# The norm ahead of the second layer in two halves: tiles 0 to 15 are normalised while tiles 16 to 31 are still being added

## The chip, the cores and the metric

The kernel runs on one core of a Trainium2 chip. The metric is the time of one execution on the device in microseconds (us). The kernel before takes 1013.03 us, the median of 3 runs (1012.9 to 1013.12).

## The reference, cut to what matters

The program is four layers of a transformer with 4096 tokens of width 128 (`x` is 64x64x128). Each layer is an attention against a context and a second part that differs from layer to layer. Around the change it computes

```
x = x + L0_attention(layernorm(x), ctx, ctx, tau, delta)     # 16 heads of width 8
x = x + L0_ffn(layernorm(x), g_info, W_qkv, W_proj, b_proj)  # self-attention over x with a class per token
```

where `layernorm(x) = (x - mean) / sqrt(var + 1e-5)` over the 128 columns of a token. The change touches the second of these norms and the step that makes the queries from it. All arithmetic stays as it is.

## The kernel before, in words

The 4096 tokens lie in the array `X` as 32 tiles of 128 tokens; four tiles are a chunk (512 tokens), so there are 8 chunks. Attention runs over 16 units of two tiles. Each engine has its own program, and the programs meet at semaphores; inside one engine the order is that of the code.

**Attention of layer 0.** In the DVE program, turn u of `attention` does the maxima and shifts of unit u, then `values(u - 1)` (reciprocal of the denominators, rows of the output), then `update(u - 2)`, which adds the projected output of two tiles to `X`, and then the statistics of two tiles (`tile_stats`, line 872) one turn later. Three more turns (u = 16, 17, 18) drain this pipe. In turn 16 DVE also does `windows()` and `guides()` (lines 846 to 864), small preparations for later layers. ACT does the exponentials and copies the turned weights and outputs out of PSUM (lines 1798, 1837, 1805); its program has turns 16 and 17. PE ends its program with 18 matmuls that compute nothing that is used (`keep_clock`, line 2077).

**The norm between.** `norms(1)` of DVE waits for the statistics of all 32 tiles, works out the variance (lines 909 to 915, five instructions of 128x32), waits for the square root of ACT (`rstds(1)`, line 1727) and makes the reciprocal root and one Newton step (lines 919 to 932). The result is a scale and a shift for each token (`rstd`, `nmr`). In front of its root ACT computes an Exp for a later layer (line 1896), and between the two stands a load of ACT's function table.

**The queries of layer 0's second part** (`prepare_own` of DVE and ACT, `prepare(1, 1, KT)` of PE). ACT normalises the four tiles of a chunk into one of two buffers (line 1741); PE turns them into the PSUM bank `psT` or `psY`, in turn (line 2115); DVE copies the bank to `KT` (line 1363); PE multiplies it by the query weights (line 2124); DVE writes the queries to `QT` (line 1367). POOL squares each chunk of queries (line 715), and when all 8 are there PE begins the classes of the tokens (line 2561).

Of the kernel before, what the change touches and what calls it, by code (L numbers as in the profile page):

```python
# [8 lines left out]
ACT = mybir.ActivationFunctionType  # L9
# [10 lines left out]
TILES = TOK // 128  # L20
CHUNK = 512
CHUNKS = TOK // CHUNK
# [6 lines left out]
WINDOW, DEV_POW = 16.0, 128.0  # L29
# [85 lines left out]
def build(nc, a, out):  # L115
    ctx = ExitStack()
    with ctx:
# [320 lines left out]
        KEEP_AT, BEST_AT, RANK_AT = {8: 0, 12: 1, 14: 2, 16: 3}, {9: 0, 13: 1, 15: 2, 17: 3}, {10: 0, 14: 1, 16: 2}  # L438
        PAIR_AT, PAIRS = 3, 15
        CHAIN_STEPS = 7  # L440
        NORM_AT = [0, 1, 2, 3, 4, 6, 7]
        gauss_ready = sem("gauss_ready")
        g_loaded = sem("g_loaded")
        sim_step = sem("sim_step")
# [375 lines left out]
        def _(v):  # L820
# [163 lines left out]
            def attention(l):  # L984
                wb = units_before[l]
                masked = l == 1

                def scores(u):
                    n = wb + u
                    sc = ps_sc[:, :].rearrange("p (r g k) -> p r g k", r=RG, k=S)  # L990
                    pr = P_s[u % 2].rearrange("p (t r i k) -> p t r i k", t=2, r=RG, k=S)
                    v.wait_ge(scores_ready, n + 1)
                    for t in range(2):
                        v.tensor_reduce(mx4[:, :, HPR * t:HPR * t + HPR], sc[:, :, HPR * t:HPR * t + HPR], AX.X,  # L994
                                        ALU.max).then_inc(max_ready, 1)
                    if masked and u >= 2:
                        mix_registers(u - 2)
                    if l == 3 and u in (4, 6, 8, 10, 12, 14):
                        four_variances((u - 4) // 2)

                    wait_reuse(v, p_turned, 4 * (n - 1))
                    for t in range(2):
                        g = slice(HPR * t, HPR * t + HPR)
                        v.wait_ge(max_ready, 2 * n + t + 1)
                        v.tensor_tensor(pr[:, t], sc[:, :, g], mx4[:, :, g].unsqueeze(3).broadcast_to([128, RG, HPR, S]),  # L1005
                                        ALU.subtract).then_inc(shifted, 1)

                def values(u):
                    n = wb + u
                    o = psT[:, 0:288].rearrange("p (g d) -> p g d", d=E + 1)  # L1010
                    v.wait_ge(pv_ready, n + 1)
                    if u < UNITS - 1:
                        keep_and_rank(u + 1)
                    v.reciprocal(rden[:, :], o[:, :, E]).then_inc(rden_ready, 1)
                    v.wait_ge(rden_ready, n + 1)

                    wait_reuse(v, o_turned, n)
                    v.tensor_tensor(o_rows[:, :].rearrange("p (g d) -> p g d", d=E), o[:, :, 0:E],
                                    rden[:, :].unsqueeze(2).broadcast_to([128, 2 * H, E]), ALU.mult).then_inc(ots_ready, 1)

                def keep_and_rank(u):
                    if l == 3 and u == UNITS - 1:
                        v.wait_ge(counted, 2)
                        v.tensor_copy(ei[:, 0, :], count_at).then_inc(place_step, 1)
                    if l == 3 and u in KEEP_AT:
                        keep_logits(KEEP_AT[u])
                    if l == 3 and u in RANK_AT:
                        rank_of(1, RANK_AT[u], rank_at(RANK_AT[u]))

                def mix_registers(u):  # L1030
                    of_reg = ots[:, :].rearrange("p (b s) -> p b s", s=S)[:, :, 0:REG]
                    v.wait_ge(o_evac, wb + u + 1)
                    v.scalar_tensor_tensor(of_reg, of_reg, 0.5, reg_out[:, UNIT * u:UNIT * u + UNIT, :],
                                           ALU.mult, ALU.add).then_inc(ots_mixed, 1)

                def update(u):
                    n = wb + u
                    t = 2 * u
                    v.wait_ge(y_ready, n + 1)
                    v.wait_ge(bo_added, TILES * l + t + 2)  # L1040
                    xt = X[:, t:t + 2, :]
                    v.tensor_tensor(xt, psY[:, 0:256].rearrange("p (t d) -> p t d", d=D), xt, ALU.add).then_inc(x_updated, 2)

                def finish_registers():
                    v.wait_ge(reg_kept, REG_STEPS)
                    v.reciprocal(reg_all[:, :, 1, :], reg_all[:, :, 1, :]).then_inc(reg_rden, 1)
                    v.wait_ge(reg_rden, 1)
                    v.tensor_tensor(reg_out[:, :, :].rearrange("p (k b) q -> p k (b q)", b=4), reg_all[:, :, 0, :],
                                    reg_all[:, :, 1, :], ALU.mult).then_inc(reg_ready, 1)
                    v.wait_ge(reg_ready, 1)  # L1050

                for u in range(UNITS + 3 if l < 3 else UNITS):
                    if u < UNITS:
                        scores(u)
                        if masked and u == 0:
                            finish_registers()
                    elif l == 0 and u == UNITS:
                        windows()
                        guides()
                    elif masked and u < UNITS + 2:  # L1060
                        mix_registers(u - 2)
                    if l == 3 and u in (4, 6, 8, 10, 12, 14):
                        four_norms((u - 4) // 2)
                    if l == 3 and u in BEST_AT:
                        best_of(1, BEST_AT[u])
                    if 1 <= u <= UNITS:
                        values(u - 1)
                    if 2 <= u <= UNITS + 1:
                        update(u - 2)
                    if l == 3 and u in RANK_AT:  # L1070
                        place(1, RANK_AT[u])
                    if l == 3 and u == UNITS - 1:
                        early_rows_table()
                    behind = 2 if l == 3 else 3
                    if behind <= u < UNITS + behind:
                        for t in (2 * (u - behind), 2 * (u - behind) + 1):
                            tile_stats(UPD_OF[l] + 1, t)
                if l == 3:
                    four_variances(6)
                    early_shifts()  # L1080
                    four_norms(6)
                return values, update
# [273 lines left out]
                unrolled(REG_STEPS, 2, step)  # L1356

            def prepare_own():

                def step(k, turn, u, live):  # L1360
                    if live(0):
                        v.wait_ge(xt_in_psum, CHUNKS + k + 1)
                        v.tensor_copy(KT[:, bass.ds(k * CHUNK, CHUNK)], (psT, psY)[u][:, :]).then_inc(xt_ready, 1)
                    if live(1):
                        r = (u + 1) % 2
                        v.wait_ge(q_proj, CHUNKS + k)
                        v.tensor_scalar(QT[:, bass.ds((k - 1) * CHUNK, CHUNK)], psS[r][:, :], bqkv[:, 1, 0:1],
                                        float(E) ** -0.5, ALU.add, ALU.mult).then_inc(q_ready, 1)

                pipeline(v, CHUNKS, 2, 1, step)  # L1370

            for t in range(TILES):
                tile_stats(0, t)
# [5 lines left out]
                            bo[:, :, :].rearrange("p l d -> p (l d)"), ALU.add).then_inc(bo_ready, 1)  # L1379
            prepare(0, 0, tau_s)  # L1380
            attention(0)
            norms(1)
            prepare_own()
            classes()
            registers()
# [50 lines left out]
            def mixture1():  # L1436
# [15 lines left out]
                                            two[:, :, NE:], be[:, :].unsqueeze(1).broadcast_to([128, 2, D]),  # L1452
                                            ALU.add).then_inc(y_kept, 1)

                v.wait_ge(norm_ready, 2 * 3 + 2)
                pipeline(v, CHUNKS, 2, 2, step)
                routing()

# [263 lines left out]
        def _(act):  # L1722
# [9 lines left out]

            def normalise(ln, k, u):

                if isinstance(k, int) and (k == 0 or k == 4 and ln in (4, 6)):
                    act.wait_ge(norm_ready, 2 * (NORM_AT[ln] + k // 4) + 2)
                wait_reuse(act, xt_in_psum, CHUNKS * ln + k - 1)
                tiles = TPC // 2 if ln in SHARED_LN else TPC
# [23 lines left out]
                act.activation(xts[s][:, :], (psT, psY)[s][:, :], ACT.Copy).then_inc(xt_ready, 1)  # L1762

            def prepare_own():
                pipeline(act, CHUNKS, 2, 0, lambda k, turn, u, live: normalise(1, k, u))

            def prepare(ln, last_keys, between=None):
                def step(k, turn, u, live):
# [22 lines left out]
            def attention(l):  # L1791
# [52 lines left out]
                for u in range(UNITS + 2 if l < 3 else UNITS + 1):  # L1844
                    if 1 <= u <= UNITS:
                        turned(u - 1)
                    elif u > UNITS:
                        outputs(u)
                    if l == 2 and u == UNITS:
                        act.preload_act_table_set("sqrt_and_others")  # L1850
                    if u < UNITS:
                        exponentials(u)

# [38 lines left out]
                    rstds(0)  # L1892
            prepare(0, lambda: take_all(0, CHUNKS - 1))
            attention(0)
            act.wait_ge(gcol_step, 2)
            act.activation(gcols[:, 1, :], gcols[:, 1, :], ACT.Exp, scale=-1.0 / DEV_POW).then_inc(gauss_ready, 1)
            rstds(1)
            prepare_own()
            classes()
            registers()  # L1900
# [169 lines left out]
        def _(pe):  # L2070
# [35 lines left out]
            def prepare(l, ln, kept=None):  # L2106
                w = W[l]

                def step(k, turn, u, live):
                    s = u % 2  # L2110
                    if live(0):
                        normalised(ln, k)
                        wait_reuse(pe, xt_ready, CHUNKS * ln + k - 1)
                        for j in range(TPC):
# [18 lines left out]
            def attention(l):  # L2133
# [134 lines left out]
                        values(u - 1, 2)  # L2268
                        values(u - 1, 3)
                if l == 0:  # L2270
                    keep_clock(psS[0], 18)
                elif l == 2:
                    pe.wait_ge(l2_loaded, 80)
                    keep_clock(psS[0], 4)
# [437 lines left out]
```

## Time and profile before

| | us |
|---|---|
| median of 3 runs | 1013.03 |
| the profiled execution, its own time | 1013.32 |
| its span | 1011.5 |
| PE busy in the span | 909.9 |
| DVE busy | 751.1 |
| ACT busy | 578.3 |

The profile is that of one execution. Starts are counted from the start of its span; what lies around the span is 1.8 us. A row of the timeline gives the start, the time from the start of the first to the end of the last of the merged instructions, the engine, the line, what is written from what, and in brackets the idle time of that engine before the row with the instruction that ended it. The stretch that the change touches goes from about 153 us (turn 16 of the attention) to 181.5 us (the classes begin).

### The profile page before, as it was taken

What the parts mean: (1) busy time and instruction counts of PE and PEld (TensorE: products, weight loads), DVE (VectorE), ACT (ScalarE), POOL (GpSimd) and SP (SyncE); (2) the same over time, 40 slices, a digit from 0 to 9 for tenths busy, and PEclk for the clock granted to TensorE, in tenths of its full rate; (3) what the DMA queues carried; (4) which work ended last, traced back from release to release, by engine and by line L of the source; (5) the groups of instructions that cost most, each with busy time, mean ns of one, the idle gap of its engine ahead of it and who ended that gap; (6) DMA issues with size and microseconds to landing.
All of it is one profiled execution on the core that took longest, in us unless ns stands there. A gap on an engine that the chain in (4) does not pass through costs nothing.

```text
span 1011.5 us, 32199 instructions
## 1 busy us (share of the span) xinstructions
PE 909.9 (90%) x12735; PEld 704.4 (70%) x12735; DVE 751.1 (74%) x1744; ACT 578.3 (57%) x1200; POOL 390.8 (39%) x435
## 2 busy tenths in 40 slices
PE   6899998988899998999987989989898998879897
PEld 3467885465777764788755857578854887668896
DVE  3588995556899956999789766556567999876664
ACT  4656666543566656666646763235485666433454
POOL 5234421335334211444202006735564435547554
PEclk9999999989999999999999999999999999798999
DMA  8399000000000000000099811122230111122221
GB/s 268 93 333 279 3 3 1 2 8 4 3 3 2 3 2 1 3 3 3 3 299 295 208 42 35 46 62 77 67 93 1 45 44 54 44 78 57 56 64 35
DMA packets 73695, 68.83 MB, mean 68 GB/s; under 512 B 7565, under 2 KB 68944, under 8 KB 73552
## 3 DMA queue, kind: packets, MB, share of 16 engines
q1 hardware_dynamic: 68336, 57.60, 20.4%
q0 software_dynamic: 4544, 8.94, 2.7%
q8 instruction: 103, 1.69, 0.7%
q14 instruction: 40, 0.33, 0.1%
q10 hardware_dynamic: 672, 0.27, 0.1%
HBM read 22.36 MB, written 44.67 MB: 66 GB/s over the span
## 4 chain that ended last, share of the span: by engine, by line
PE 28%; DVE 12%; issue 4%; ACT 3%; another core or an unknown queue 1%; POOL 1%; DMA 1%; DVEq 1%; POOLq 0%; SPq 0%; ACTq 0%
PE ps_sc L2517 7%; PE ps_pt L2525 4%; PE ps_sc L2452 2%; DVE work L1005 2%; PE ps_pt L2461 1%; PE ps_pt L2178 1%; PE psT L2192 1%; DVE stats L872 1%; DVE mx L994 1%; PE ps_sc L2166 1%; PE ps_pt L2093 1%; PE ps_sc L2088 1%; POOL xs_dram L703 1%; PE ps_pt L2443 1%
## 5 line engine op out<-in xcount | busy, mean ns | idle before, releaser
L1837 ACT ACTIVATE P_t<-ps_pt 128x512 f32<-128x512 f32 x256 | 140.0, 594 | 146.6 <-PE ps_pt L2178 140.2
L994 DVE TENSOR_REDUCE mx<-ps_sc 128x16 f32<-128x1024 f32 x128 | 150.2, 1215 | 19.4 <-PE ps_sc L2166 19.2
L2192 PE MATMUL psT<-VB,P_t 128*64 128x18 f32 x4096 | 145.3, 213 | 13.7 <-ACT P_t L1837 6.3
L2192 PEld LDWEIGHTS psT<-VB,P_t 128*64 128x64 f32 x4096 | 131.9, 138 | 35.6 <-ACT P_t L1837 25.8
L1005 DVE TENSOR_TENSOR work<-ps_sc,mx 128x1024 f32<-128x1024 f32 x128 | 150.1, 1214 | 0.0
L1798 ACT ACTIVATE work<-work 128x1024 f32<-128x1024 f32 x128 | 130.9, 1058 | 27.9 <-DVE work L1005 26.2
L2178 PE MATMUL ps_pt<-cst,work 128*128 128x128 f32 x1024 | 142.2, 283 | 0.0
L2178 PEld LDWEIGHTS ps_pt<-cst,work 128*128 128x128 f32 x1024 | 112.2, 143 | 26.7 <-ACT work L1798 20.6
L656 POOL TENSOR_TENSOR kbh<-KT,cst 128x512 f32<-128x512 f32 x64 | 65.3, 1042 | 134.7 <-PE ps_sc L2166 93.8
L656 POOL TENSOR_TENSOR rt<-KT,cst 128x512 f32<-128x512 f32 x64 | 65.5, 1045 | 101.5 <-PE ps_sc L2166 101.5
L2517 PE MATMUL ps_sc<-kbh,KT 128*128 128x128 f32 x624 | 89.4, 289 | 2.1 <-DVE kbh L1633 1.2
L2517 PEld LDWEIGHTS ps_sc<-kbh,KT 128*128 128x128 f32 x624 | 79.8, 200 | 6.7 <-DVE kbh L1633 3.6
L2043 ACT ACTIVATE P_t<-ps_sc,KT 128x128 f32<-128x128 f32 x156 | 44.6, 368 | 55.0 <-PE ps_sc L2517 47.8
L2525 PE MATMUL ps_pt<-VB,P_t 128*128 x468 | 68.4, 284 | 6.5 <-DVE P_t L1638 5.2
L2525 PEld LDWEIGHTS ps_pt<-VB,P_t 128*128 128x128 f32 x468 | 60.7, 198 | 8.8 <-issue 8.4
L663 POOL TENSOR_TENSOR x_rows<-x_rows,bo 128x256 f32<-128x256 f32 x64 | 43.5, 683 | 45.7 <-issue 26.4
L872 DVE BATCH_NORM_STATS2 stats<-x_rows 128x6 f32<-128x128 f32 x256 | 56.9, 280 | 4.4 <-DMA x_rows<-x_in 3.7
L703 POOL DMA_INDIRECT xs_dram<-QT,dest x32 | 31.1, 973 | 70.3 <-issue 68.3
L797 POOL DMA_INDIRECT ys_dram<-work,to_row x39 | 37.9, 973 | 39.8 <-DVE to_row L1626 19.2
L1605 DVE COPY KT<-VB 128x512 f32 (+1 forms) x78 | 34.8, 446 | 23.4 <-ACT P_t L2043 16.6
L799 POOL DMA_INDIRECT out<-work,to_row x39 | 39.0, 1000 | 34.0 <-issue 16.5
L1741 ACT ACTIVATE work<-x_rows,nmr,rstd 128x128 f32<-128x128 f32 (+1 forms) x112 | 46.8, 483 | 7.1 <-DVE nmr L932 3.0
(374 smaller groups left out, 1716.9 us busy)
## 6 DMA issues: line engine op xcount, KB each, us to landing
xs_dram<-slots SPq DMA_DIRECT2D x1, 17292.0 KB, 71.0
xs_dram<-slots SPq DMA_DIRECT2D x1, 17160.0 KB, 58.6
ctxT<-xs_dram SPq DMA_DIRECT2D x39, 65.5 KB
work<-xs_dram SPq DMA_DIRECT2D x39, 65.0 KB
VB<-L_ffn_W1b_in SPq DMA_DIRECT2D x8, 258.0 KB
ctxT<-ctxT_in SPq DMA_DIRECT2D x4, 512.0 KB, 6.9
x_rows<-x_in SPq DMA_DIRECT2D x4, 512.0 KB, 9.2
QT<-ys_dram SPq DMA_DIRECT2D x4, 512.0 KB, 6.1
```

Source lines behind the costliest of these rows:

```text
L656: pool.tensor_tensor(by_head[:, 2 * h:2 * h + 2, :, :], KT[:, at:at + 2 * S].rearrange("p (b k) -> p b k", k=S).unsqueeze(2).broadcast_to( ...
L872: v.bn_stats(stats[:, bass.ds(t, 1), :].rearrange("p o c -> p (o c)"), X[:, bass.ds(t, 1), :].rearrange("p o d -> p (o d)")).then_inc(stat ...
L994: v.tensor_reduce(mx4[:, :, HPR * t:HPR * t + HPR], sc[:, :, HPR * t:HPR * t + HPR], AX.X, ALU.max).then_inc(max_ready, 1)
L1005: v.tensor_tensor(pr[:, t], sc[:, :, g], mx4[:, :, g].unsqueeze(3).broadcast_to([128, RG, HPR, S]), ALU.subtract).then_inc(shifted, 1)
L1741: act.activation(xn[u][:, j, :], X[:, bass.ds(t, 1), :].rearrange("p o d -> p (o d)"), ACT.Identity, bias=nmr[:, bass.ds(t, 1)], scale=rst ...
L1798: act.activation(half_p, half_p, ACT.Exp).then_inc(exp_ready, 1)
L1837: act.activation(P_t[:, 512 * c:512 * c + 512], ps_pt[:, 512 * (c % 2):512 * (c % 2) + 512], ACT.Copy).then_inc(p_evac, 1)
L2043: done = act.activation(hT[s][:, cols], psS[s][:, cols], ACT.Relu, bias=w_tile[s][:, 512 + j:513 + j])
L2178: mm = pe.transpose(ps_pt[:, 512 * (c % 2) + 128 * r:512 * (c % 2) + 128 * r + 128], P_s[u % 2][:, at:at + 128], ident)
L2192: mm = pe.matmul(psT[64 * b:64 * b + 64, 144 * t + 18 * g:144 * t + 18 * g + 18], P_t[:, at:at + 64], VB[:, UNIT * u + 2 * t + b, g, :, :] ...
L2517: mm = pe.matmul(psS[r][:, 128 * b:128 * b + 128], w_tile[r][:, 128 * b:128 * b + 128], xT[r], start=True, stop=True)
L2525: mm = pe.matmul(psO[s][:, 0:128], hT[s][:, 128 * b:128 * b + 128], wv[:, bass.ds(e_back * F + (w_out_at + 128 * b), 128)], start=(b == 0) ...
```

## The change

The norm is made in two halves. The variance of tiles 0 to 15 is worked out in turn 16 of the attention, ahead of `windows()`, and its reciprocal root at the end of that turn, ahead of the last `update`. ACT's Exp, the table load and the root of the first half move up into turn 16, ahead of the last copy of outputs. The variance of tiles 16 to 31 comes where `norms(1)` stood; its root is taken by ACT between chunks 1 and 2, and its reciprocal root by DVE between the copies of chunks 0 and 1. ACT waits for the second half at chunk 4. `prepare_own` is unrolled on both engines. PE waits for the end of `psT`'s use ahead of chunk 0 and for the last `update` ahead of chunk 1 (these hold `psT` and `psY`), and its `keep_clock` behind the attention goes from 18 matmuls to 6. The numbering of the norms' semaphores moves by one for the later norms.

```diff
-        NORM_AT = [0, 1, 2, 3, 4, 6, 7]
+        NORM_AT = [0, 1, 3, 4, 5, 7, 8]
 # DVE, attention
                 for u in range(UNITS + 3 if l < 3 else UNITS):
+                    if l == 0 and u == UNITS:
+                        finish_first = norms_of(1, slice(0, TILES // 2), 0)
                     if u < UNITS:
                         scores(u)
...
                         for t in (2 * (u - behind), 2 * (u - behind) + 1):
                             tile_stats(UPD_OF[l] + 1, t)
+                    if l == 0 and u == UNITS:
+                        finish_first()
 # DVE, prepare_own
+                finish_second = norms_of(1, slice(TILES // 2, TILES), 1)
+
+                def take_own(k, u):
+                    v.wait_ge(xt_in_psum, CHUNKS + k + 1)
+                    v.tensor_copy(KT[:, bass.ds(k * CHUNK, CHUNK)], (psT, psY)[u][:, :]).then_inc(xt_ready, 1)
+
+                take_own(0, 0)
+                finish_second()
...
-                    if live(0):
-                        v.wait_ge(xt_in_psum, CHUNKS + k + 1)
-                        v.tensor_copy(KT[:, bass.ds(k * CHUNK, CHUNK)], (psT, psY)[u][:, :]).then_inc(xt_ready, 1)
+                    if live(0) and k > 0:
+                        take_own(k, u)
...
-                pipeline(v, CHUNKS, 2, 1, step)
+                unrolled(CHUNKS, 1, step)
...
             attention(0)
-            norms(1)
             prepare_own()
 # ACT
-                if isinstance(k, int) and (k == 0 or k == 4 and ln in (4, 6)):
+                if isinstance(k, int) and (k == 0 or k == 4 and ln in (1, 4, 6)):
...
-                pipeline(act, CHUNKS, 2, 0, lambda k, turn, u, live: normalise(1, k, u))
+                for k in range(CHUNKS):
+                    normalise(1, k, k % 2)
+                    if k == 1:
+                        root_of(1, slice(TILES // 2, TILES), 1)
...
-                    if l == 2 and u == UNITS:
+                    if l == 0 and u == UNITS:
+                        act.wait_ge(gcol_step, 2)
+                        act.activation(gcols[:, 1, :], gcols[:, 1, :], ACT.Exp, scale=-1.0 / DEV_POW).then_inc(gauss_ready, 1)
+                    if l in (0, 2) and u == UNITS:
                         act.preload_act_table_set("sqrt_and_others")
+                    if l == 0 and u == UNITS:
+                        root_of(1, slice(0, TILES // 2), 0)
...
             attention(0)
-            act.wait_ge(gcol_step, 2)
-            act.activation(gcols[:, 1, :], gcols[:, 1, :], ACT.Exp, scale=-1.0 / DEV_POW).then_inc(gauss_ready, 1)
-            rstds(1)
             prepare_own()
 # PE, prepare
                     if live(0):
+                        if l == 1 and isinstance(k, int) and k == 0:
+                            pe.wait_ge(ots_ready, UNITS)
+                        elif l == 1 and isinstance(k, int) and k == 1:
+                            pe.wait_ge(x_updated, TILES)
                         normalised(ln, k)
 # PE, end of attention
                 if l == 0:
-                    keep_clock(psS[0], 18)
+                    keep_clock(psS[0], 6)
```

## Rows read from the trace of the kernel before

**Rows 1.** Chain that ended last: shares of the span by engine.

```profile
PE 28%; DVE 12%; issue 4%; ACT 3%; another core or an unknown queue 1%; POOL 1%; DMA 1%; DVEq 1%; POOLq 0%; SPq 0%; ACTq 0%
```

**Rows 2.** Timeline of ACT, 155 to 190 us: start, length, work, idle before.

```profile
155.94 1.08 ACT L1837 ACTIVATE P_t<-ps_pt 128x512 f32<-128x512 f32 x2 [1.04 <-PE ps_pt L2178]
159.62 0.38 ACT L1805 ACTIVATE oh<-psY 128x256 f32<-128x256 f32 x1 [2.59 <-PE psY L2203]
159.90 0.22 ACT L1896 ACTIVATE gcols<-gcols 128x32 f32<-128x32 f32 x1
160.14 1.28 ACT L1727 ACT_TABLE_LOAD   x1
162.93 0.23 ACT L1727 ACTIVATE lnw<-lnw 128x32 f32<-128x32 f32 x1 [1.51 <-DVE lnw L915]
164.48 7.94 ACT L1741 ACTIVATE work<-x_rows,nmr,rstd 128x128 f32<-128x128 f32 x20 [1.32 <-DVE nmr L932]
172.90 4.73 ACT L1741 ACTIVATE work<-x_rows,nmr,rstd 128x128 f32 x12 [0.47 <-PE psY L2115]
```

**Rows 3.** Timeline of DVE, 153 to 185 us.

```profile
157.88 0.36 DVE L1014 RECIPROCAL rden<-psT 128x32 f32<-128x32 f32 x1 [2.82 <-PE psT L2192]
...
158.94 0.48 DVE L872 BATCH_NORM_STATS2 stats<-x_rows 128x6 f32<-128x128 f32 x2
160.86 0.43 DVE L1042 TENSOR_TENSOR x_rows<-psY,x_rows 128x256 f32<-128x256 f32 x1 [1.44 <-issue]
161.20 0.86 DVE L872 BATCH_NORM_STATS2 stats<-x_rows 128x6 f32<-128x128 f32 x4
162.10 0.22 DVE L909 TENSOR_TENSOR lnw<-stats 128x32 f32<-128x32 f32 x1
...
164.25 0.19 DVE L932 SCALAR_TENSOR_TENSOR nmr<-lnw,rstd 128x32 f32<-128x32 f32 x1
166.88 0.69 DVE L1363 COPY KT<-psT 128x512 f32<-128x512 f32 x1 [2.44 <-PE psT L2115]
```

**Rows 4.** Timeline of PE, 157 to 186 us.

```profile
160.60 4.05 PE L2077 MATMUL ps_sc<-cst 128*128 128x512 bf16 x18
166.18 0.66 PE L2115 MATMUL psT<-cst,work 128*128 128x128 f32 x4 [1.53 <-ACT work L1741]
...
169.48 1.06 PE L2115 MATMUL psT<-cst,work 128*128 128x128 f32 x4
170.34 1.88 PE L2124 MATMUL ps_sc<-KT,W 128*128 x2
...
178.28 1.02 PE L2124 MATMUL ps_sc<-KT,W 128*128 x2
...
181.54 1.92 PE L2561 MATMUL ps_sc<-QT,gate 128*32 128x512 f32 x16 [0.73 <-DVE QT L1367]
```

**Rows 5.** PE by stretches: length, busy (x instructions), granted clock, DMA share, GB/s.

```profile
165.24:168.65 3.41, 1.59 (x10) 1.00 0.00 0
168.65:172.06 3.41, 3.41 (x9) 0.50 0.00 0
...
202.78:206.20 3.42, 0.80 (x22) 1.00 0.05 8
206.20:209.61 3.41, 3.19 (x69) 0.50 0.05 8
```

**Rows 6.** Timeline of DVE, 758 to 762 us: the same chain over 16 tiles.

```profile
760.08 0.24 DVE L919 RECIPROCAL lnw<-lnw 128x16 f32<-128x16 f32 x1
...
760.99 0.17 DVE L932 SCALAR_TENSOR_TENSOR nmr<-lnw,rstd 128x16 f32<-128x16 f32 x1
```

**Rows 7.** ACT at other places: roots of 16 tiles (min/median/max ns); a table load.

```profile
L1731 ACT ACTIVATE lnw<-lnw x4: 198/216/217, 543.0 to 759.0; 128x16 f32<-128x16 f32 x4
...
600.09 1.28 ACT L2002 ACT_TABLE_LOAD   x1 [1.31 <-DVE nmr L932]
601.39 1.65 ACT L1989 ACTIVATE QT<-x_rows,nmr,rstd 128x128 f32<-128x128 f32 x4
```

More of the change, by code:

```diff
@@ L1453, in step @@
                                             ALU.add).then_inc(y_kept, 1)
-                v.wait_ge(norm_ready, 2 * 3 + 2)
+                v.wait_ge(norm_ready, 2 * NORM_AT[3] + 2)
                 pipeline(v, CHUNKS, 2, 2, step)
```

## The prediction

> **What bounds the kernel now.** I read the chain of waits first. PE has the largest share of it, 28%, DVE 12% and ACT 3% [rows 1], so no single engine is the bound everywhere and the stretch has to be read for itself. I then read the three timelines from turn 16 of the attention to the start of the classes.
>
> The stretch is one chain. The last two tiles are added at 160.86 us; four statistics follow (161.20), the variance (162.10), ACT's root (162.93 to 163.16), and the Newton step ends at 164.25 + 0.19 = 164.44 [rows 2, 3]. ACT starts on the first tile at 164.48, released by `nmr`, and is then busy nearly without a gap: 20 tiles in 7.94 us, 0.47 us idle, 12 tiles in 4.73 us, so its last tile ends at 177.63 [rows 2]. The classes start on PE at 181.54, released by the last queries of DVE; that is 3.91 us behind ACT's last tile [rows 4]. So ACT, at 0.397 us for a tile and 1.59 us for a chunk, sets the pace here, and the end of the stretch is the start of ACT's stream plus its work plus a tail. No tile of the first 16 needs anything that happens after 159.42, the end of the statistics of turn 16 (158.94 + 0.48) [rows 3]. The wait is one for all statistics, not one for data.
>
> **The change part by part.**
>
> First variance (five instructions, DVE, turn 16). With 32 tiles it takes from 162.10 to the start of ACT's root at 162.93, 0.83 us [rows 2, 3]; half as many columns won't take longer. It stands ahead of `windows()`, and DVE is idle for 2.82 us at the end of that work, until PE has the last values at 157.88 [rows 3]. 0.83 fits in 2.82, so it costs nothing; without that cover it would cost at most 0.83. Behind it on DVE stand `windows()` and `guides()`, and ACT's Exp waits for two of these; ACT is free only at 155.94 + 1.08 = 157.02 [rows 2], later than they are done.
>
> Exp, table load and first root (ACT, turn 16). Exp takes 0.22, the load 1.28 [rows 2], a root over 16 tiles 0.22 [rows 7]: 1.72 us, say 1.8 with the gaps. ACT is idle for 2.59 us from 157.02 until the turned outputs of the last unit release it at 159.62 [rows 2]. So it is done at about 158.8, with 0.8 to spare. Behind these three waits the last copy of outputs, and for that copy wait PE's projection and the last update: each us beyond the cover is paid in full.
>
> The Trainium skill, "ScalarE: Activation LUTs", section "What ACT_TABLE_LOAD costs", speaks against this fit: a switch of the set costs the load and a drain of about 1.38 us, 2.66 us in all. The rows do not show such a drain: behind the load at 600.09, 1.28 long, the next activation starts at 601.39 [rows 7]. By the page ACT would be done at 157.02 + 0.22 + 2.66 + 0.22 = 160.12, past its cover, and the gain would be some 0.7 us smaller; this is a rival below, worked there from the rows.
>
> First reciprocal root (five instructions, DVE). Over 16 tiles it goes from 760.08 to 760.99 + 0.17, 1.08 us [rows 6]. It starts behind the statistics of turn 16, at 159.42 + 0.04, and ends at 160.54. DVE is idle there for 1.44 us, until the last update at 160.86 [rows 3], so this is hidden too, with 0.3 to spare; the update does not move. Nothing else waits behind it.
>
> Start of ACT's stream. It becomes 160.54 + 0.04 = 160.58 instead of 164.48: 3.90 us earlier. ACT has by then done its last copy of outputs (159.62 + 0.38 = 160.00) [rows 2]. This is the main term.
>
> Second half. Its variance comes where the old one stood, 162.10 to at most 162.93 [rows 3], while ACT works on chunks 0 and 1 until 160.58 + 8 x 0.397 = 163.76. ACT then takes the second root, 0.22 us, less a few hundredths by which activations overlap: I charge 0.20. DVE copies chunk 0 at about 163.0, waits for the root until 164.0 and has the second half at 165.1. So its copy of chunk 1, which could have started at 166.88 + 1.53 - 3.90, about 164.5, is 0.6 to 0.7 late. What hides this: the next work of PE is to turn chunk 2, which ACT finishes only at 163.96 + 1.59 = 165.55; the copy (0.69 us [rows 3]) is through at 165.8, and the projection of chunk 1 stands behind the turning in any case. Without that cover it costs 0.7. ACT needs the second half for chunk 4, at 163.96 + 3.18 = 167.1, two us after it is there.
>
> PE. Its new waits are for the last rows of outputs, made before the statistics at 158.94, and for the last update, at 160.86 + 0.43 = 161.29 [rows 3], both before chunk 0 is normalised (160.58 + 1.59 = 162.17). `keep_clock` must shrink for this: 18 matmuls take 4.05 us from 160.60 [rows 4] and would hold PE until 164.65; 6 take 1.35 and end at 161.95, 0.2 ahead of chunk 0. PE then waits as it did before, from chunk to chunk.
>
> The clock of PE. In the stretch 165.24 to 168.65 PE was busy for 1.59 of 3.41 us, and in the next one the granted clock was 0.50, the lower level of 1.2 GHz [rows 5]. There, turning a chunk takes 1.06 instead of 0.66 and projecting it 1.88 instead of 1.02 us [rows 4], together 2.94, more than ACT's 1.59; ACT's idle 0.47 us [rows 2], ended by PE's turning, is what came of it. In the changed kernel the gap behind the last `keep_clock` matmul is 0.2 to 0.4 us instead of 1.53, so PE has more to do in such a stretch. I take it that the clock stays at 2.4 GHz here and the 0.47 us go; at the other end they stay.
>
> Unrolled loops. ACT's 0.397 us for a tile holds across its loop and the part in front of it [rows 2], so the loop cost nothing that could be won; I set 0, between -0.1 and 0.1.
>
> Numbers of the norms' semaphores: 0, a constant in an instruction that is there anyway.
>
> Sum: 3.90 - 0.20 + 0.47 = 4.17 us; 3.70 if the idle time stays. Behind 181.54 all waits for the last queries [rows 4], so I carry the gain to the end at its full size. From the profiled execution, 1013.32 - 4.17 = 1009.15; its time is 0.29 above the median of the runs, so for the median 1013.03 - 4.17 = 1008.86, **1008.9 us**.
>
> **The rivals.**
>
> The clock falls at the new place, for longer. With 12 matmuls fewer PE may be found too little busy while chunks 0 and 1 come in, and run the next chunks at 1.2 GHz, two low stretches instead of one. Each holds 3.41/2.94, about 1.2 chunks, each 1.35 us over ACT's pace: 1.6 us a stretch, of which before only 0.47 came through since the other engines had slack. For two I take 3.2 less 1.2 of slack, 2.0 us, from a base of 4.17: gain 2.2, 1010.8 us. For it speaks that the first pair of chunks still leaves PE idle for some 0.9 us of each 1.59 (turning takes 0.66) [rows 4]; against it that the long gap is gone.
>
> The table load holds ACT for longer than it shows. If the root comes out at 160.12, DVE makes the first half from 160.16 to 161.24, ACT starts at 161.28, 0.70 later than forecast, and the update, 0.5 late, lies beside that. Gain 3.5, 1009.5 us. Against it stands the load with an activation 0.02 us behind it [rows 7].
>
> The clock further down. All that follows moves by 4 us, and the gaps of PE that cost it the clock later, such as 0.80 busy of 3.42 us ahead of the fall at 206.20 [rows 5], fall differently. One low stretch more or less, with PE at the bound, is worth up to half of its 3.41 us, 1.7 us either way: 1007.2 or 1010.6 us.
>
> The gain does not arrive. Should something that the change does not move set the start of the classes or of what follows them, the time stays 1013.0. Against it: PE's wait at 181.54 was ended by DVE's queries, and nothing else is named there [rows 4].
>
> The other side: PE stays at 1.2 GHz through the whole preparation, because with waits at every chunk it is never busy enough to be given 2.4 GHz. It would cost 8 chunks x 1.35 = 10.8 us against the forecast, 1019.7 us. It decides from about three chunks on (4.17/1.35). Against it: at the low clock PE was busy for 3.41 of 3.41 us, and the clock rose at once [rows 4, 5]: a slower PE has no gaps here.
>
> **How the numbers follow.** Forecast 0.60; longer fall of the clock 0.15; table load 0.05; clock further down by more than 1 us 0.12 (half to each side); gain does not arrive 0.05; PE slow throughout 0.03. The forecast's own range is 1008.4 to 1009.5 (the idle 0.47 stays or goes, 0.1 for loops). To leave out no more than 2 in 10 I go from 1007.5 to 1011.0: below it half of the better cases further down, above it the last two rivals and part of two others. A measurement of this kernel can tell about 0.2%, 2.0 us, from no change: faster means under 1011.0. Forecast, table load, nearly all of the clock cases: faster 0.85; within 0.2%: 0.11, the gain that does not arrive and the worse ends of the clock cases; slower 0.04.
>
> **What would show it.** Right: ACT's Exp, load and root lie between 157.0 and 158.9 and the copy of outputs still starts at about 159.6; the last update stays at 160.9; ACT's first tile starts at about 160.6, its last ends at 173.5; the classes start at 177.4; PE's clock is 1.00 from 161 to 177. Wrong: a copy of outputs after 159.8 (load), a clock of 0.50 for more than 3.4 us before 177 (PE), an idle gap of ACT behind the second root, or a start of the classes at 177.4 with a span that is not 4 us shorter (further down).

## The result, and the profile after

The changed kernel takes 1006.09 us, the median of 20 executions (1001.78 to 1012.69). The kernel before, measured beside it, takes 1009.61 us, also of 20 (1006.95 to 1015.23); the three runs that the prediction started from are among these. The ratio is 0.9961, with a 95% interval of 0.9943 to 0.9978: faster by 0.4%. (The ratios in this document are those of the measurement; the quotient of the two medians, here 0.9965, can differ from them by up to 0.0016.) The forecast was 1008.9 us in a range from 1007.5 to 1011.0; the measured median lies below it. The forecast as a ratio, 1008.86/1013.03 = 0.9959, was met. One execution in the whole study, of the kernel late_half below, was slow (1447.36 us at a mean granted clock of 0.548); it is left out of that kernel's median and ratio.

The profiled execution of the changed kernel took 1002.57 us (span 1000.8), 10.7 us less in span than the one of before. The timeline of ACT from 154.9 us on (start, length, work, idle before) answers to [rows 2]:

```profile
154.98 1.28 ACT L1866 ACT_TABLE_LOAD   x1
156.27 0.22 ACT L1741 ACTIVATE lnw<-lnw 128x16 f32<-128x16 f32 x1
157.43 0.38 ACT L1818 ACTIVATE oh<-psY 128x256 f32<-128x256 f32 x1 [0.95 <-PE psY L2222]
158.26 3.19 ACT L1751 ACTIVATE work<-x_rows,nmr,rstd 128x128 f32<-128x128 f32 x8 [0.44 <-DVE nmr L932]
161.35 0.20 ACT L1741 ACTIVATE lnw<-lnw 128x16 f32<-128x16 f32 x1
161.46 9.33 ACT L1751 ACTIVATE work<-x_rows,nmr,rstd 128x128 f32<-128x128 f32 x24
```

Load and root lie ahead of the copy of outputs at 157.43, with 0.95 us to spare. The stream of tiles has no idle time: it ends at 161.46 + 9.33 = 170.79. DVE, against [rows 3]:

```profile
155.69 0.36 DVE L1014 RECIPROCAL rden<-psT 128x32 f32<-128x32 f32 x1 [2.21 <-PE psT L2211]
...
158.05 0.18 DVE L932 SCALAR_TENSOR_TENSOR nmr<-lnw,rstd 128x16 f32<-128x16 f32 x1
158.68 0.43 DVE L1042 TENSOR_TENSOR x_rows<-psY,x_rows 128x256 f32<-128x256 f32 x1 [0.45 <-PE psY L2233]
...
160.68 0.69 DVE L1367 COPY KT<-psT 128x512 f32<-128x512 f32 x1
161.59 0.25 DVE L919 RECIPROCAL lnw<-lnw 128x16 f32<-128x16 f32 x1 [0.22 <-ACT lnw L1741]
...
162.59 0.69 DVE L1367 COPY KT<-psY 128x512 f32<-128x512 f32 x1
```

The first half is ready at 158.23, 0.45 us ahead of the last update, which is still released by PE's projection. PE, against [rows 4]:

```profile
158.42 1.46 PE L2092 MATMUL ps_sc<-cst 128*128 128x512 bf16 x6
160.01 0.63 PE L2134 MATMUL psT<-cst,work 128*128 128x128 f32 x4
161.55 0.63 PE L2134 MATMUL psY<-cst,work 128*128 128x128 f32 x4 [0.91 <-issue]
...
163.22 0.65 PE L2134 MATMUL psT<-cst,work 128*128 128x128 f32 x4 [0.19 <-ACT work L1751]
163.71 1.02 PE L2143 MATMUL ps_sc<-KT,W 128*128 x2
...
174.30 1.92 PE L2580 MATMUL ps_sc<-QT,gate 128*32 128x512 f32 x16 [0.73 <-DVE QT L1378]
```

The stretches of PE (length, busy and instructions, granted clock, DMA) answer to [rows 5]: the fall in the preparation is gone, the one at the register step is still there.

```profile
158.50:161.91 3.41, 2.37 (x15) 1.00 0.00 0
161.91:165.33 3.42, 3.23 (x16) 1.00 0.00 0
...
197.20:200.61 3.41, 1.77 (x66) 1.00 0.05 8
200.61:204.02 3.41, 3.06 (x41) 0.50 0.06 12
```

From the last update to the start of the classes it is 174.30 - 158.68 = 15.62 us, in place of 181.54 - 160.86 = 20.68 us: **5.06 us less**, where 4.17 were forecast. The rest of the 10.7 us is not the change: 2.18 us lie ahead of the last update (158.68 against 160.86). They are there before the first added instruction: DVE's reciprocal of the turn before, ahead of which neither order nor work differs, starts at 149.68 against 151.87. About 1.0 us of it is there at 33 us, and 1.3 us more at 40 us, behind a low stretch of PE's clock at 35.53 that only the profile of before has. The other 3.46 us lie behind the start of the classes (826.50 us to the end against 829.96).

### The profile page after: what moved, and what is told of

It reads as the page before. It is cut to its first block, busy times and chain, and to the rows that moved or that the text cites. A ratio compares the mean times of both kernels' runs of the same rounds, so it can differ in the third digit from the quotient of the medians.

```text
span 1000.8 us, 32098 instructions
## 1 busy us (share of the span) xinstructions
PE 900.1 (90%) x12723; PEld 696.8 (70%) x12723; DVE 753.5 (75%) x1754; ACT 577.5 (58%) x1201; POOL 391.1 (39%) x435
## 4 chain that ended last, share of the span: by engine, by line
PE 28%; DVE 12%; issue 4%; ACT 3%; POOL 1%; another core or an unknown queue 1%; DMA 1%; DVEq 1%; POOLq 0%; SPq 0%; ACTq 0%
PE ps_sc L2536 7%; PE ps_pt L2544 4%; PE ps_sc L2471 2%; DVE work L1005 2%; PE psT L2211 2%; DVE mx L994 2%; PE ps_pt L2480 1%; DVE stats L872 1%; PE ps_pt L2197 1%; PE ps_sc L2185 1%; PE ps_pt L2108 1%; PE ps_sc L2103 1%; POOL xs_dram L703 1%; PE ps_pt L2462 1%
## 5 line engine op out<-in xcount | busy, mean ns | idle before, releaser
L2536 PEld LDWEIGHTS ps_sc<-kbh,KT 128*128 128x128 f32 x624 | 77.7, 196 | 9.1 <-DVE kbh L1643 4.9
```

The costliest lines, as they stand in the source:

```text
L2536: mm = pe.matmul(psS[r][:, 128 * b:128 * b + 128], w_tile[r][:, 128 * b:128 * b + 128], xT[r], start=True, stop=True)
```

## The experiments

They ran on two chips: the first four kernels below "changed, first profile" on one on which the kernel before takes 993.02 us (median of 35 executions), the last four on one on which it takes 992.40 us (23). The comparison is in each case with the kernel before on the same chip in the same session. Each kernel has 12 executions, but fill_after 6 and unroll_only 1. "Local" is the time from the start of the last update to the start of the classes in the profiled execution, as above; ACT's start is counted from that update, the stream is ACT's 32 tiles, the tail the time from their end to the classes.

| kernel | median us | ratio to before (95%) | ACT's start | stream | tail | local |
|---|---|---|---|---|---|---|
| before, first profile | 1009.61 | | +3.62 | 13.15 | 3.91 | 20.68 |
| changed, first profile | 1006.09 | 0.9961 (0.9943 to 0.9978) | -0.42 | 12.53 | 3.51 | 15.62 |
| again_before | 992.42 | 1.0007 (0.9988 to 1.0025) | +3.62 | 13.14 | 3.91 | 20.67 |
| again_after | 988.53 | 0.9951 (0.9927 to 0.9975) | -0.41 | 12.52 | 3.52 | 15.63 |
| keep18 | 989.23 | 0.9970 (0.9949 to 0.9990) | -0.42 | 14.02 | 3.53 | 17.13 |
| keep6_only | 993.31 | 1.0008 (0.9985 to 1.0030) | +3.62 | 13.41 | 3.89 | 20.92 |
| late_half | 992.64 | 1.0001 (0.9979 to 1.0023) | +3.21 | 13.79 | 3.72 | 20.72 |
| unroll_only | 995.26 (one) | | +3.62 | 12.43 | 3.51 | 19.56 |
| fill_before | 988.23 | 0.9952 (0.9929 to 0.9974) | +3.63 | 13.13 | 3.92 | 20.68 |
| fill_after | 983.14 | 0.9891 (0.9863 to 0.9919) | -0.42 | 12.53 | 3.52 | 15.63 |

**again_before and again_after: the two kernels as they are.**

> The kernel before, unchanged. Theory (clock): where the low stretches of PE's clock fall differs from execution to execution, and with them the time; so the ratio to itself is 1.000 within 0.002, single executions spread over some 5 to 8 us, a profile with fewer low stretches than the 11 of the first one is shorter by about half of the low time it saves, and the local stretch (last update of layer 0 to the start of the classes) is 20.7 us with a low stretch in it and about 19.8 us without. Rival (the time is fixed by the work, and 1013.03 us was its level): executions within 0.3 us of 1013, and a profile with low stretches at the same places, 35.5, 168.7, 206.2 us and so on.

> The changed kernel, unchanged. Theory (clock): ratio 0.996 again (0.9945 to 0.9975), the local stretch is 15.6 us (last update 158.68 to classes 174.30) if no low stretch falls in it, and the span differs from 1000.8 us by about 0.5 us for each us of low clock more or less. Rival (the first profile was 10.7 us shorter because of the change): a span of 1000.8 within 0.5 us again and a ratio near 0.989.

The local stretch came back to 0.01 us in both. The spans did not: single executions of before went from 988.51 to 997.34 us (35 of them), of the changed kernel from 982.44 to 992.91 (12). The profiled spans, 991.8 and 989.0, differ by 2.8 us, less than the 5.04 of the local stretch, since the rest was 2.0 us longer in the changed kernel (814.77 against 812.79). The row "PEclk" of the page, tenths of the full clock in 40 slices, shows more low clock in the changed kernel; first again_before, then again_after:

```profile
PEclk9999999979799999999999999999999999988899
```

```profile
PEclk9999999989799999999999999999999999788899
```

Behind the classes the clock was low for 44.4 us in again_before and 51.2 us in again_after, summed over stretches as in [rows 5] and without the last one, in which the execution ends. In the first pair it was 41.0 and 30.7 us, and there the changed kernel's rest was the shorter one by 3.46. So the ratio and the local stretch came out as the theory had them, and the rival (10.7 us from the change) fell. One part of both expectations is not met. By the clock alone again_before should have taken about as long as the first profile of before (0.974 against 0.975), and again_after some 10 us more than 1000.8 (0.972 against 0.982); they were 19.7 and 11.8 us shorter. The two profiles of before are within 0.5 us of each other up to the experts of layer 2, at 650 us. Some 10 us of the difference lie in these experts, about as much behind 830 us. The first store and the last of the 39 tiles of layer 2's experts, in the first profile of before and in again_before:

```profile
L797 POOL DMA_INDIRECT ys_dram<-work,to_row x39: 956/960/1118, 669.6 to 735.9; - x39
```

```profile
L797 POOL DMA_INDIRECT ys_dram<-work,to_row x39: 953/959/1163, 670.1 to 725.9; - x39
```

They are 66.3 us apart in the one, 55.8 in the other; the changed kernel has 66.3 (first profile) and 56.0 (again_after). That follows the chip or the session, not the kernel.

**keep18: the filler behind the attention as long as before.**

```diff
-                    keep_clock(psS[0], 6)
+                    keep_clock(psS[0], 18)
```

> The changed kernel with 18 matmuls of keep_clock behind the first attention in place of 6. Theory: PE is held until 158.4 + 4.05 = 162.5 in place of 159.9, chunk 0 is turned about 2.5 us later (162.5 in place of 160.0), ACT has both its buffers full at 161.4 and waits about 1.2 us for the first to be turned; the local stretch grows by 1 to 1.6 us, ratio to before 0.997 to 0.998. Rival (the shorter keep_clock costs as much clock as it saves time): the local stretch is not longer than 15.6 us, ratio 0.996 or less.

As expected, the stretch growing by 1.50 us: ACT fills both buffers, takes the second root and then waits for PE, which has been held by the filler. ACT, then PE:

```profile
161.11 0.20 ACT L1741 ACTIVATE lnw<-lnw 128x16 f32<-128x16 f32 x1
162.70 9.34 ACT L1751 ACTIVATE work<-x_rows,nmr,rstd 128x128 f32<-128x128 f32 x24 [1.39 <-PE psT L2134]
```

```profile
158.18 4.05 PE L2092 MATMUL ps_sc<-cst 128*128 128x512 bf16 x18
162.07 0.60 PE L2134 MATMUL psT<-cst,work 128*128 128x128 f32 x4
```

The shorter filler is worth 17.13 - 15.63 = 1.5 us of the 5.06, and without it the ratio is 0.9970 in place of 0.9951 (the intervals overlap; the profile is what decides).

**keep6_only: the shorter filler without the early start.**

> The kernel before with the one edit that keep_clock behind the first attention has 6 matmuls in place of 18. Theory: nothing is gained since chunk 0 is only there at 166.1 us and PE idles 4.2 us in place of 1.5; the clock falls in the preparation of the queries in most executions, so ratio 1.000 to 1.002, local stretch 20.7 to 22 us. Rival (part of the gain is the shorter filler itself): ratio 0.998 or less.

The stretches of PE behind the filler:

```profile
162.49:165.90 3.41, 1.69 (x7) 0.50 0.00 0
165.90:169.31 3.41, 3.41 (x10) 0.50 0.00 0
```

Two low stretches in place of one, local 20.92 against 20.67, ratio 1.0008, as expected. Alone the edit gives nothing: it is worth something only once chunk 0 is there sooner. ACT's stream, whose loop is not unrolled here, is of use further down:

```profile
162.09 6.27 ACT L1741 ACTIVATE work<-x_rows,nmr,rstd 128x128 f32<-128x128 f32 x16 [1.32 <-DVE nmr L932]
169.23 6.27 ACT L1741 ACTIVATE work<-x_rows,nmr,rstd 128x128 f32 x16 [0.87 <-PE psT L2115]
```

**late_half: halves, unrolled loops and short filler, but the first half behind the attention.**

```diff
-                    if l == 0 and u == UNITS:
-                        finish_first = norms_of(1, slice(0, TILES // 2), 0)
...
-                    if l == 0 and u == UNITS:
-                        finish_first()
...
+                norms_of(1, slice(0, TILES // 2), 0)()
                 finish_second = norms_of(1, slice(TILES // 2, TILES), 1)
```

(On ACT the Exp, the table load and the first root go back behind the attention likewise.)

> The changed kernel with only the early move undone: the norm is still in two halves, the loops are unrolled and keep_clock has 6 matmuls, but the variance, the table load, the root and the reciprocal root of the first half come behind the attention. Theory (the early start of ACT's stream is the gain): variance, root and reciprocal root of 16 tiles take 2.1 us behind the last statistics, so ACT starts 3.3 to 3.4 us behind the start of the last update in place of 0.42 us ahead of its start; the local stretch is 19.3 to 20 us in place of 15.6, ratio 0.998 to 1.000. Rival (halves, unrolling and filler make the gain): ratio 0.996.

ACT's start moves by 3.63 us, from -0.42 to +3.21, and the whole gain is gone: local 20.72, ratio 1.0001. The early start itself accounts for 3.63 of the 5.09 us; the other 1.46 lie in the stream and the tail and go with two low stretches, which the expected 19.3 to 20 us did not have, and for which that range was missed. The root now stands behind the last statistics:

```profile
160.82 0.21 ACT L1738 ACTIVATE lnw<-lnw 128x16 f32<-128x16 f32 x1 [1.27 <-DVE lnw L915]
162.19 3.19 ACT L1748 ACTIVATE work<-x_rows,nmr,rstd 128x128 f32<-128x128 f32 x8 [1.16 <-DVE nmr L932]
...
169.22 1.65 ACT L1748 ACTIVATE work<-x_rows,nmr,rstd 128x128 f32<-128x128 f32 x4 [0.66 <-PE psT L2129]
171.25 4.73 ACT L1748 ACTIVATE work<-x_rows,nmr,rstd 128x128 f32<-128x128 f32 x12 [0.38 <-PE psY L2129]
```

The two waits for PE, 0.66 and 0.38, are the low clock again, from 163.75 to 170.58 us.

**unroll_only: the loops of the preparation unrolled, nothing else.**

> The kernel before with the preparation of layer 0's queries unrolled on DVE and ACT and nothing else. Theory: the loop costs ACT a few hundredths of a us at each tile of chunks 2 to 7: the 32 tiles take 12.5 us without idle time in place of 12.7, and the local stretch is 20.4 us with a low stretch of the clock in it, 19.6 without. Rival (unrolling also takes away the 0.4 us by which the queries of the last chunk were late): the time from ACT's last tile to the classes is 3.5 us in place of 3.9 even with a low stretch.

In this execution no low stretch fell into the preparation. ACT:

```profile
162.81 12.43 ACT L1741 ACTIVATE work<-x_rows,nmr,rstd 128x128 f32<-128x128 f32 x32 [1.32 <-DVE nmr L932]
```

The numbers expected for an execution without a low stretch came, 12.43 and 19.56, but the reason given for them, a cost of the loop at each tile, is not in the rows. Without a wait a tile starts every 0.385 us and lasts 0.48, so a row of n tiles is about (n - 1) x 0.385 + 0.48 long: 12.42 for these 32, 6.26 for each 16 of keep6_only, whose loop is not unrolled and takes 6.27. The loop costs ACT nothing. What unroll_only saves against before, 13.15 - 12.43 = 0.72 us, lies in two places of before's low stretch: the tile at 170.77 starts 0.12 late, a delay too short to be shown as a wait, and the one at 172.90 starts 0.57 late, which the row gives as 0.47 of idle time; tiles in a row overlap by 0.1 us, and a wait loses that too.

The tail is 3.51, without the early start; so its 0.40 us do not come from the early start. How much of them is the low stretch and how much the unrolling is not separated. With two low stretches the tail is 3.89 in keep6_only (loops) and 3.72 in late_half (unrolled), unrolled without one it is 3.51 to 3.53; loops without a low stretch were never seen.

**fill_before and fill_after: PE kept busy in four waits.**

```diff
                 mask(0)
+                keep_clock(psY[:, :], 10)
...
-                        keep_clock(psO[1], 18)
+                        keep_clock(psO[1], 24 if masked else 18)
...
-                        keep_clock(psP[1], 4)
+                        keep_clock(psP[1], 16 if k == 1 else 4)
...
                 for k in range(tiles + 2):
+                    if k == 0:
+                        keep_clock(psS[1], 14)
```

> The kernel before with matmuls that compute nothing put into four waits of PE that stand ahead of a fall of its clock: 10 behind the first mask of the register step, 6 more at the start of the second attention, 12 more in the third attention's second step, 14 ahead of the last experts. Theory (the scatter of the times is PE's clock, which falls after stretches with waits): mean granted clock up from 0.979 to 0.985 or more, the low stretches at about 204, 258 and 558 us gone in the profile, ratio 0.994 to 0.998, spans over a range of 5 us or less in place of 9. Rival (the scatter is something else, such as the loads from memory): clock up but ratio 1.000 within 0.002 and the range as before. Other side (the filler holds up real matmuls): ratio over 1.002.

> The changed kernel with the same four fillers. Theory (the two edits are in different stretches and add up): ratio of the changed kernel, 0.995, times that of fill_before; 0.989 to 0.993, the fastest of all kernels here, clock 0.985 or more. Rival (part of the gain of the change is clock further down, which the fillers give to both kernels): the distance between fill_after and fill_before is under 3 us, in place of the 5.0 us by which the local stretch is shorter.

Both are faster than before, by 0.48% and by 1.09%. In the profile of fill_before the low stretches at about 204, 258 and 558 us are gone, but two others, at 588.95 and 664.04, are there. The mean clock of all their executions is 0.989 and 0.991 against 0.979 for before. PE by windows, first again_after, then fill_after:

```profile
200.00:210.00 10.00, 9.61 (x257) 0.66 0.06 11
250.00:260.00 10.00, 8.47 (x111) 0.59 0.01 2
545.00:555.00 10.00, 7.07 (x45) 0.86 1.10 286
```

```profile
200.00:210.00 10.00, 9.29 (x345) 1.00 0.06 12
250.00:260.00 10.00, 9.46 (x199) 1.00 0.01 3
545.00:555.00 10.00, 9.91 (x75) 1.00 1.10 281
```

The medians of the two kernels stand 5.1 us apart and their profiled local stretches 5.05, so the change keeps its worth when the clock further down is cared for; against the rival's 3 us this speaks clearly, though six executions of fill_after are few. The scatter is a partial miss: fill_after's spans lie within 3.9 us (6 executions), fill_before's still over 9.6 us (982.1 to 991.7). fill_after is the fastest kernel of the study.

## Why the prediction was wrong

**The mechanism, and its steps.** ACT's stream set the end of the stretch and its start was bound by a wait for all statistics: shown by late_half, where ACT starts 3.63 us later and the classes with it. The covers held: first variance (DVE was still idle for 2.21 us), load and root (0.95 us to spare), reciprocal root (0.45 us to spare), new waits of PE (none shows as a wait). The copy of chunk 1 was late, at 162.59 while its turning had ended at 162.18, and hidden behind the turning of chunk 2 at 163.22, as said. The rival of the table load fell: the root starts 0.01 us behind the load. The Trainium skill's further 1.38 us ("ScalarE: Activation LUTs", "What ACT_TABLE_LOAD costs") are not there in these rows; the trace decides. The filler had to shrink: 1.5 us.

**The sum.** Forecast 4.17, measured 5.06:

| term | forecast | measured | from |
|---|---|---|---|
| start of ACT's stream | 3.90 | 4.04 | +3.62 to -0.42 |
| second root in the stream | -0.20 | -0.10 | 12.53 against 12.43 (unroll_only) |
| ACT's waits at the low clock | 0.47 | 0.72 | 13.15 against 12.43 (unroll_only) |
| loops, on ACT | 0 | 0 | keep6_only, unroll_only |
| tail | 0 | 0.40 | 3.91 to 3.51 |

The start was 0.14 better since the reciprocal root starts ahead of the end of the statistics (157.15 against 156.76 + 0.48). The second root cost 0.10 in place of 0.20 for the same reason for which a wait costs 0.1 more than it shows: instructions of ACT in a row overlap by 0.1 us, where the prediction took a few hundredths. Its 0.397 us for a tile is a mean with one hidden delay in it; the pace is 0.385. The tail is the term that was left out, 0.40, part of it a delay of PE and DVE that lasted from the low stretch to the last chunk. So the idle time of 0.47 was not all that the low stretch cost. The lower end of the forecast's own range, 1008.4, does not follow from its terms: 0.1 for the loops gives 1008.8.

**The level: the step that failed.** "So for the median 1013.03 - 4.17 = 1008.86" took the median of three runs as the level of the kernel. The three agreed within 0.22 us, and the prediction read that as the scatter. The 20 executions of before run from 1006.95 to 1015.23, with a median 3.4 us lower. With 1009.61 as the base, 4.17 us less are 1005.4; measured 1006.09. So of the 2.77 us by which the forecast was too high, the level makes 3.42, and the difference of the medians, 3.52 in place of 4.17, takes 0.65 back. That the ratio was met is in part luck: forecast with a base that was too high and a local gain that was 0.9 too low, and measured with an interval of 0.0035, which can't tell 4.17 from 5.06.

**The size of the clock's share.** The rival "the clock further down" priced one low stretch, 1.7 us either way, and its place in the range was half a chance on each side. In fact low stretches come and go by several at a time. Of the 20 executions of the changed kernel the five fastest (1001.78 to 1002.86 us) have mean granted clocks of 0.979 to 0.982, the four slowest (1012.22 to 1012.69) all 0.971. From the fastest to the slowest the low time, twice the missing share of the span, grows from 2 x 0.020 x 1000.0 = 40 to 2 x 0.029 x 1010.8 = 59 us, and the span by 10.8 us. Over all 20 the two go together with a correlation of 0.95, over the 35 of before in the second session 0.80. That the clock makes most of the scatter rests on these correlations. The fillers show by intervention that more granted clock goes with shorter kernels; they did not make fill_before's scatter smaller, so it is not shown that the clock makes all of it.

The falls, such as those at 168.65 and 206.20 us [rows 5], are no fixed part of the kernel: in the first profile of before the one in the preparation comes 7.8 us behind the last update, in again_before 7.5 us, in unroll_only not at all, and behind the classes before was at the low clock for 41.0 us in one profile and 44.4 in the other. The Trainium skill states that the monitor behind the clock runs free and does not start anew with the kernel ("TensorE: Matmul & The Clock Gate", "What's actually happening"). These pairs agree with that, but no run here moved the kernel against the clock and nothing else. The prediction used the fall as if it were part of the kernel.

**What stays open.** Why the kernel before has a median some 17 us lower in the later sessions (its profiles are 20 us apart, 10 us of it in the experts of layer 2) was not tried; the change has no part in it, but a time in us is not carried from one session to another. Whether the gain is 3.9 us (0.9961, first session) or 4.9 (0.9951, again_after) the intervals do not tell; the local 5.06 lies in both. How the 0.40 us of the tail divide between the low stretch and the unrolling is open too.

## What to carry to other kernels

A reduction over all tiles ahead of a stage that takes them one by one is a barrier; splitting it pays as much as the stage's own stream can start sooner, provided that the small steps find idle gaps on each engine and that any filler behind the barrier is shortened with it. Give a forecast as a difference or a ratio, read the scatter from the mean granted clock of many executions rather than from three that agree, and put that scatter into any range in us. Where PE waits ahead of a fall of its granted clock, a few matmuls that compute nothing can be worth as much as a reordering: here 0.5% for four such places. They must end before the real work is there: 12 too many cost 1.5 us in keep18.

## What the runs showed of the hardware that was not expected

Two profiles of the same kernel had the clock fall at the same time, 251.81 and 251.79 us, and in one it stayed low for 3.4 us, in the other for 10.2, though PE was busy for 9.79 of the 10.24 us. The stretches of PE, in again_after and in the first profile of the changed kernel:

```profile
251.79:262.03 10.24, 9.79 (x102) 0.50 0.01 2
```

```profile
251.81:255.22 3.41, 3.41 (x45) 0.50 0.02 5
255.22:258.60 3.38, 3.35 (x55) 1.00 0.00 0
```

So the same kernel, with PE busy in both, had the full clock back after 3.4 us in one execution and after 10.2 in the other.

A fall did not always follow idle time of PE either. In again_before PE was busy throughout the 3.41 us ahead of the one at 913.31, mostly with matmuls of only 8 and 32 columns, and for 3.19 of the 3.41 us ahead of these:

```profile
909.90:913.31 3.41, 3.41 (x34) 1.00 0.23 64
913.31:916.73 3.42, 3.42 (x19) 0.50 0.21 60
```

So PE's busy time alone, by which the prediction judged where the clock would fall, does not tell it.

Each us of low clock went with 0.46 us of span in the first session (20 executions of the changed kernel), with 0.28 and 0.38 in the two later ones (35 and 23 of before). That all are under half fits a PE that is the bound in only part of the low time; it was not tested, and the recorded clock, rounded to 0.001, gives the low time of an execution to 2 us only.
